# Post-norm transformer layer on one core: output projection and first norm of a query chunk moved into the next chunk's attention, result writes moved to GpSimd's queue, down products by whole chunks

## The reference

```python
Q, K, V = X @ Wq + bq, X @ Wk + bk, X @ Wv + bv
attn = softmax(q @ k.T / sqrt(16)) @ v                 # b, h, query, d
out  = attn.transpose(0, 3, 2, 1).reshape(b, s, 256)   # b, d, query, h, read as rows of 256
x = layernorm(X + out @ Wo + bo)
x = layernorm(x + ((silu(x @ Wg * sg) * (x @ Wu * su)) @ Wd) * sd)
```

## Time and profile before

| | us |
|---|---|
| median of 3 timed runs | 707.35 (707.09 to 709.0) |
| the profiled execution's own time | 709.39 |
| its span, first to last instruction | 707.6 |
| TensorE busy (matmul) | 630.2 |
| ScalarE busy | 545.9 |
| VectorE busy | 141.5 |
| GpSimd busy | 54.2 |
| mean granted clock of TensorE, as a share of full | 0.943 |

### The profile page before, as it was taken

The page is one execution under the profiler, slowest core; times in us unless marked ns, Lnnn a source line. Parts: engine busy times, 40 slices in busy tenths (PEclk is TensorE's granted clock), DMA queues, the critical chain, the costliest instruction groups (busy, mean ns, idle before and its releaser), DMA issues.

```text
span 707.6 us, 9879 instructions
## 1 busy us (share of the span) xinstructions
PE 630.2 (89%) x3938; PEld 260.8 (37%) x3938; DVE 141.5 (20%) x266; ACT 545.9 (77%) x637; POOL 54.2 (8%) x49
## 2 busy tenths in 40 slices
PE   8999999999998969998999699898959709999994
PEld 6862222222222212222222122222212108788884
DVE  6680000000000100000010000000100005856766
ACT  4639999999997969997999499899958802744442
POOL 7445000000000000000000000000012001000002
PEclk9999999999998979998999799999988958999998
DMA  7646739383749475573838293848371020000001
GB/s 226 106 64 77 78 42 102 35 100 37 87 55 96 45 79 58 66 82 42 100 53 94 31 107 36 92 51 97 39 88 12 6 38 0 1 1 30 0 30 60
DMA packets 55836, 43.21 MB, mean 61 GB/s; under 512 B 43320, under 2 KB 49336, under 8 KB 52912
## 3 DMA queue, kind: packets, MB, share of 16 engines
q1 hardware_dynamic: 54976, 42.35, 47.8%
q10 hardware_dynamic: 816, 0.26, 0.1%
HBM read 6.56 MB, written 4.33 MB: 15 GB/s over the span
## 4 chain that ended last, share of the span: by engine, by line
PE 57%; SPq 28%; DMA 5%; DVE 4%; issue 3%; ACT 2%; POOL 0%; ACTq 0%; DVEq 0%; POOLq 0%
PE ps L1043 22%; PE ps L1027 18%; SPq L286 10%; SPq L289 7%; PE ps L1111 7%; PE ps L908 5%; SPq L299 4%; SPq L297 4%; PE ps L1094 4%; SPq L312 3%; DMA q_slot<-shift 2%; PE ps L1082 2%; DMA at_dram<-attn_q 1%; ACT probs L519 1%; DVE attn_q L692 1%
## 5 line engine op out<-in xcount | busy, mean ns | idle before, releaser
L519 ACT ACTIVATE probs<-ps 128x1024 f32<-128x1024 f32 x512 | 472.0, 1317 | 54.4 <-PE ps L1027 54.2
L1043 PE MATMUL ps<-probs,v_all 128*17 128x512 f32 x2048 | 279.6, 619 | 1.7 <-DVE attn_q L692 1.1
L1027 PE MATMUL ps<-q_slot,k_slot 51*128 51x512 f32 x1024 | 230.4, 498 | 38.5 <-DMA q_slot<-shift 36.9
L1027 PEld LDWEIGHTS ps<-q_slot,k_slot 51*128 51x128 f32 x1024 | 94.5, 190 | 310.7 <-ACT probs L519 259.6
L692 DVE COPY attn_q<-ps 128x512 f32<-128x512 f32 x16 | 11.1, 691 | 490.0 <-PE ps L1043 490.0
L1043 PEld LDWEIGHTS ps<-probs,v_all 128*17 128x17 f32 x2048 | 34.3, 96 | 75.9 <-issue 64.2
L554 ACT ACTIVATE sg<-ps,sgate_c 128x512 f32<-128x512 f32 x32 | 22.1, 690 | 46.6 <-PE ps L1111 46.5
L444 POOL CAST wg<-gate 128x2048 fp32r<-128x2048 int8 x1 | 1.9, 1889 | 458.3 <-DMA q_slot<-shift 458.3
L1082 PE MATMUL ps<-wo,at 128*128 128x256 f32 x64 | 16.8, 428 | 21.9 <-DVE at L700 21.9
L531 ACT ACTIVATE x_tok<-x_tok,neg_mean,rstd 128x256 f32<-128x256 f32 x16 | 8.3, 590 | 35.1 <-DVE neg_mean L741 35.1
L1094 PE MATMUL ps<-wd,h_hi 128*128 128x256 f32 x128 | 32.2, 285 | 2.3 <-DVE r_tmp L773 2.1
(11 more groups left out here) (94 smaller groups left out, 326.5 us busy)
## 6 DMA issues: line engine op xcount, KB each, us to landing
k_slot<-k_parts SPq DMA_DIRECT2D x60, 256.0 KB
k_slot<-k_parts SPq DMA_DIRECT2D x60, 128.0 KB
q_slot<-q_parts SPq DMA_DIRECT2D x64, 64.0 KB
at_dram<-attn_q SPq DMA_DIRECT2D x64, 34.0 KB
at<-at_dram SPq DMA_DIRECT2D x8, 272.0 KB, 5.0
q_slot<-q_parts SPq DMA_DIRECT2D x64, 32.0 KB
x_tok<-in_L_attn_X SPq DMA_DIRECT2D x3, 512.0 KB, 9.0
out<-out_tmp SPq DMA_DIRECT2D x3, 512.0 KB, 3.0
```

Source lines behind the costliest of these rows:

```text
L519: nc.scalar.activation(probs[:, u % 3, 2 * p:2 * p + 2, :].rearrange("p a b -> p (a b)"), ps[:, 2 * ring:2 * ring + 2, :].rearrange("p a b ...
L1027: last = nc.tensor.matmul(ps[:, 2 * ring + half, :], k_slot[slot][base:base + ROWS, p, kt * P:(kt + 1) * P], q_slot[slot][base:base + ROWS ...
L1043: last = nc.tensor.matmul(ps[32 * hh:32 * hh + VW, ACC, :], v_all[:, kt, NQ * (s % QUADS) + hh, :], probs[:, u % 3, hh, :], start=(kt == 0 ...
```

## The change

- Result writes `move_out` are issued by GpSimd instead of SyncE. SyncE keeps `load_stack`, `load_shift` and `move_in`; `move_in(c)` moves up to the end of the iteration of the chunk's last step.
- Tokens lie otherwise on the partitions: x_tok's row (d % 4)*32 + u and column block j, c hold token j*512 + (d % 4)*128 + 32c + u, so that a chunk of queries makes whole tiles of 128 tokens. Each chunk of X is loaded by 4 DMAs of 32 partitions instead of one (two for the first) of 128; each result chunk is stored by 4.
- Chunks 0 to 2: `project_out(c, b)` runs on TensorE in units 4 and 7 of step 4c+5, and `turn_y(c, ko)` in units 4 and 7 of step 4c+6, all through bank 7. VectorE does `scale_attn`, sums, statistics and now also the scaling of the first norm after the save of step 4c+4, and both parts of the turned tile after the save of step 4c+5. GpSimd does the power between two result writes. The normed, turned chunk takes the place of Q's chunk (`qy`).
- Chunk 3: `scale_attn` after feed-forward tile 7 on VectorE, `project_out` before tile 10 and `turn_y` before tile 13 on TensorE, the VectorE parts in between.
- The feed-forward begins when attention ends. All 8 down products of a chunk run together after its 8 tiles of gate and up. `ln2_step` runs at tiles 0 to 4 of the next chunk, with two VectorE instructions instead of four in its first piece.
- The loops of the feed-forward are written out, the last stores are shared by SyncE and ScalarE.

The core of the diff:

```diff
@@ sync
+            def load_x(j):
+                for d in range(CH):
+                    sp.dma_start(x_tok[UW * d:UW * (d + 1), TPC * j:TPC * (j + 1), :], x_view[j, d]
+                                 ).then_inc(x_loaded[j], 16)
...
-                if s >= QUADS and s % QUADS == 0:
-                    move_in(s // QUADS - 1)
-                sp.wait_ge(attn_saved, s + 1)
-                move_out(s)
-            move_in(CH - 1)
+                if s % QUADS == QUADS - 1:
+                    move_in(s // QUADS)
@@ gpsimd
+            def move_out(s):
+                c = s // QUADS
+                pool.wait_ge(attn_saved, s + 1)
+                for hh in range(NQ):
+                    pool.dma_start(at_dram[c, :, NQ * (s % QUADS) + hh, :, :].rearrange("r d u -> d r u"),
+                                   attn_q[s % 2][32 * hh:32 * hh + VW, :, :]).then_inc(at_put[s % 2], 16)
...
+            for s in range(STEPS):
+                if s > QUADS and s % QUADS == 1:
+                    ln1_power(s // QUADS - 1)
+                if s == STEPS - 1:
+                    for t in range(STEPS - NSLOT, STEPS):
+                        pool.wait_ge(stack_loaded[t % NSLOT], loaded(t))
+                    nc.gpsimd.tensor_copy(wg[:], gate8[:].bitcast(i8)).then_inc(ffn_w_ready, 1)
+                    ...
+                move_out(s)
+            ln1_power(LAST)
@@ vector
+            for s in range(STEPS):
+                save_attn(s)
+                c = s // QUADS - 1
+                if s >= QUADS and s % QUADS == 0:
+                    scale_attn(c)
+                    ln1_add(c, 0)
+                    ln1_add(c, 1)
+                    ln1_stats(c)
+                    ln1_scale(c)
+                if s >= QUADS and s % QUADS == 1:
+                    ln1_parts(c, 0)
+                    ln1_parts(c, 1)
@@ tensor, attention
+                s, kt = u // UPS, u % UPS
+                c = s // QUADS - 1
+                if c >= 0 and s % QUADS == 1 and kt in (4, 7):
+                    project_out(c, kt // 7)
+                if c >= 0 and s % QUADS == 2 and kt in (4, 7):
+                    turn_y(c, kt // 7)
@@ tensor, feed-forward
+            for u in range(CH * MT):
+                c, m = u // MT, u % MT
+                if u == WO_AT:
+                    project_out(LAST, 0)
+                    project_out(LAST, 1)
+                if u == TURN_AT:
+                    turn_y(LAST, 0)
+                    turn_y(LAST, 1)
...
+                if u >= 2:
+                    pe.wait_ge(gate_up_free, u - 1)
...
+                if m == MT - 1:
+                    for b in range(c * MT, (c + 1) * MT):
                         down(b)
```

More of the change, by code:

```diff
@@ L438, in _, with ln1_power @@
                                         ).then_inc(bo_added, 1)
[L441 to L449, removed]
+            def move_out(s):
[4 more added lines that the diff above has]
+                                   attn_q[s % 2][32 * hh:32 * hh + VW, :, :]).then_inc(at_put[s % 2], 16)
+            def ln1_power(c):
                 pool.wait_ge(ln1_var, c + 1)
@@ L540, in _ @@
[L540 to L543, removed]
-            act.wait_ge(scales_loaded, 16 * 3)
[L547 to L567, removed]
@@ L1046, in prob_times_v, with project_out, turn_y @@
                 last.then_inc(pv_done, 1)
+            def project_out(c, b):
+                bank = FFN_BANK if c < LAST else 6 + b
+                if b == 0:
+                    pe.wait_ge(attn_scaled, c + 1)
+                if c == 0 and b == 0:
+                    pe.wait_ge(w_loaded[3], 16)
+                if b == 0 and c == LAST:
+                    pe.wait_ge(down_free, 2)
+                if b == 0 and c:
+                    pe.wait_ge(yt_ready, KO * c)
+                if b == 1 and c < LAST:
+                    pe.wait_ge(ln1_sum, 2 * c + 1)
+                for half in range(2):
+                    j = 2 * b + half
+                    for ko in range(KO):
+                        last = nc.tensor.matmul(ps[:, bank, half * HID:(half + 1) * HID],
+                                                at32[:, c, ko, CH * j:CH * (j + 1), :].rearrange("p d u -> p (d u)"),
+                                                wo[:, ko, :], start=(ko == 0), stop=(ko == KO - 1))
+                last.then_inc(wo_psum, 1)
+            def turn_y(c, ko):
+                bank = FFN_BANK if c < LAST else 6 + ko
+                if ko == 0:
+                    pe.wait_ge(ln1_ready, TPC * (c + 1))
+                elif c < LAST:
+                    pe.wait_ge(yt_ready, KO * c + 1)
+                for j in range(TPC):
+                    last = nc.tensor.transpose(ps[:, bank, j * P:(j + 1) * P], x_by[:, j, c, ko * P:(ko + 1) * P],
+                                               ident[:])
+                last.then_inc(yt_psum, 1)
             UNITS = UPS * STEPS
@@ L1133, in _ @@
-            ffn_chunk(0, True)
-            with pe.Fori(1, CH) as c:
-                ffn_chunk(c, False)
-            for m in range(MT - LAG, MT):
-                pe.wait_ge(h_ready, (CH - 1) * MT + m + 3)
-                down(m)
+            for u in range(CH * MT):
+                c, m = u // MT, u % MT
+                if u == WO_AT:
+                    project_out(LAST, 0)
[3 more added lines that the diff above has]
+                    turn_y(LAST, 1)
+                if m == 0 and c < LAST:
+                    pe.wait_ge(yt_ready, KO * (c + 1))
+                if u >= 2:
+                    pe.wait_ge(gate_up_free, u - 1)
+                for w, bank in ((wg, u % 2), (wu, 2 + u % 2)):
+                    for ko in range(KO):
+                        for part in range(2):
+                            last = nc.tensor.matmul(ps[:, bank, :], w[:, ko, m * P:(m + 1) * P], qy[:, c, ko, part, :],
+                                                    start=(ko == 0 and part == 0), stop=(ko == KO - 1 and part == 1))
+                last.then_inc(gate_up_psum, 1)
+                if m == MT - 1:
+                    for b in range(c * MT, (c + 1) * MT):
+                        down(b)
```

361 lines of the change are left out of this document (146 added, 215 removed).

## The result

The change makes the kernel slower: a median of 721.08 us (718.83 to 725.35, 4 runs) against 707.76 for the kernel before on the same chip, a ratio of 1.0193, 95% interval 1.0142 to 1.0244. The forecast was 639.4 us and the range ended at 670. The profiled execution took 718.83 us, with a span of 717.1.

What follows compares the result with a forecast made beforehand. SyncE's queue, with a 32.0 us period, was taken to starve attention steps wanting 29.33. Terms -43.0 + 6.9 - 32.8 + 1.0 = -67.9 took 707.35 us to 639.4, range 631 to 670.

Steps and rivals of the forecast that it cites:

- Part 1: Attention: with result writes off SyncE's queue, stacks come in time and steps take 29.33 us; -43.0 us.
- I take the spread: Attention's writes spread over four or more DMA engines, the busiest has at most 23.4 us per step, ScalarE stays the bound.
- The slower one: Rival in attention: GpSimd's issue, over 8.6 us per write, becomes the bound and the kernel gets slower; chance 0.04.
- The writes still load one engine or queue: Rival in attention: moved writes still load one DMA engine or queue, steps stay at 32 us, 675.5 us total; chance 0.12.
- Part 2: Projection and turn of chunks 0 to 2 inside attention: insertions cost 1.0 and 1.3 us per chunk, +6.9 us.
- Part 3: Last save to last down product: chunks of 22.4, 32.6, 24.0 and 24.0, 103.0 us instead of 135.8, so -32.8.
- Part 4: Kernel start: SyncE issues 11 more DMAs, so X and Wk come later; +1.0 us, bounds 0 and 3.

Runs made afterwards that it cites:

- b_sp16: The kernel before, with only SyncE's result writes of 17 partitions split into four of 16 and one of 4 per step: 654.4 us, 0.9241.
- a_sp16: The changed kernel with result writes back on SyncE, split into four of 16 partitions and one of 4 per step: 641.4 us, 0.9054.
- best2: a_sp16 with chunk 3's projection moved before feed-forward tiles 4, 6 and 10, and ScalarE making the turned tile's high part: 642.01 us, 0.9064.

## Why the prediction was wrong

**What bounds the kernel before.** It was right that a 32.0 us period of SyncE's queue starves steps of 29.33. What was missed is why: the four writes hold the queue 9.1 us and the load behind them another 2.5 because of their shape. With 16 partitions per write the same kernel has its 29.33 back (b_sp16), on the same queue. The 1.4 engines that the writes kept busy were read, and led only to the question of who else uses that engine, not to the question why 136 KB load one engine.

**Part 1, the step that failed: "I take the spread".** The price of one issue, about SyncE's 2.2 us, was right (1.9), but not that four take 9: with the hold before a later one they take up to 28 (27.4 in the rows above). The error that costs the time is that a spread divides a fixed 20 us of engine time among more engines. On GpSimd's queue the sum itself grows, from 20 to 187 us with the writes alone and 136 per step beside the loads. The bound there, 23.4 us for the busiest engine, held that sum fixed. With the measured sums, spread evenly over 16 engines, a step has (289 + 136) / 16 = 26.6 us for each, and at the share of 0.82 that the stretch shows this is 32.4 us, where the loads' period is 32.4 to 34.6. That the loads wait for engines which the writes hold is inferred from these sums; no view here shows single engines. Term: -43.0 forecast; with the insertions' -36.1, against +31.4 measured. That is 67.5 of the 81.7 us by which the forecast is off (721.08 against 639.4). The 18.4 us "of every engine" was a sum of packet times too, which can overlap, and so no firm floor for the stack.

The Trainium skill ("DMA: Bandwidth & Descriptors", "Why a DMA increments its semaphore by 16 and not by 1") takes the largest number up to 16 that divides the outer dimensions as the number of engines: 1 for 17 and 19, 9 for 18, 10 for 20. The runs sort in that way (and as even and odd), and on SyncE 17 partitions at a share of 1.4 engines and 20 at 9.4 are near it. For some copies that GpSimd issues the Trainium skill names there an exception, all engines with the partitions divided by 16 and rounded up on each; which of the two the writes of 17 take, the trace doesn't tell, since packets overlap in its shares. The Trainium skill states no price there, and the runs' is 187 against 20 us. The Trainium skill says on the same page ("Issuing engines are not separate DMA queues") that a second issuer saves only issue time and that all run on the same 16 engines; here the loads, on another queue, slowed down with the writes, which agrees.

That the shape is the cause is shown from both sides, and with this shape alone the issuer matters: on GpSimd 16, 18 and 20 partitions give 641.6, 640.99 and 640.92 us, 17 and 19 give 721.08 and 755.91; on SyncE 17 gives 679.09 and 16 or 20 give 641.4 and 641.05.

**The rivals.** The slower one named 34.3 us per step as the point where the gain is gone, and 34.3 was measured; that the kernel is 14 us slower there comes from the other terms below, and the equal number is chance. Its mechanism was not the one: an issue takes 1.9 us and not over 8.6, and GpSimd still waits 131.9 us in 16 waits for saves, so it isn't the bound. The 0.04 was too little because the price's bound "by what makes it the limit" was named and then set aside for the nearest row, which was of another queue. "The writes still load one engine or queue" was nearer in kind (transfers, not issue), but it held the total fixed too and ended at 675.5.

**Part 2, insertions: right within 0.35 us.** Forecast were 1.0 and 1.3 us. ScalarE around the two in the changed kernel:

```profile
227.22 5.61 ACT L532 ACTIVATE probs<-ps 128x1024 f32<-128x1024 f32 x6 [1.43 <-PE ps L1011]
234.08 12.02 ACT L532 ACTIVATE probs<-ps 128x1024 f32<-128x1024 f32 x13 [1.25 <-PE ps L1011]
```

In a_sp16 a step with them is 31.98 - 29.33 = 2.65 us longer, 8.0 for three chunks against 6.9. Its 15 steps take 446.5 us; the forecast's 483.0 - 36.1 is 446.9. That they agree to 0.4 is in part luck: the insertions cost 1.1 more than forecast, and the last step is 27.98 instead of 29.33.

**Part 3, after attention: right where its condition held.** It needed chunk 3's result 22 us after the last save. In the changed kernel it came at 625.79, 30 us after. The chain that ended last (start, us, what):

```profile
596.87 5.73 POOL at_dram L445 x3
602.60 11.78 issue
614.38 8.03 DMA at_dram<-attn_q
...
622.85 2.92 DMA at<-at_dram
...
625.79 0.56 DVE den L689
...
628.91 5.61 PE ps L1051 x16
```

So this stretch took 111.3 us instead of 103.0. In a_sp16, where nothing is late, the four down blocks are these (start, us, of the chain):

```profile
542.43 7.67 PE ps L1113 x64
...
574.68 8.05 PE ps L1113 x64
...
598.79 7.67 PE ps L1113 x64
...
622.48 7.21 PE ps L1113 x60
```

By their ends, and to the last down product at 629.87, the chunks take 22.6, 32.6, 23.7 and 23.4 us from the last save, 102.4 together (their sum differs by rounding); forecast were 22.4, 32.6, 24.0 and 24.0. Chunk 1's long stay is VectorE's chain of first norm, second norm and `h`, as forecast: best2, which takes the first norm out of it, brings it to 24.9.

**Part 4, start.** +2.1 us against +1.0, within its bounds of 0 and 3; in the other runs of the changed kernel +1.5 to +3.2. The first transposes wait 2.43 us for X (0.86 before) and the first products are slow, 1.20 us instead of 0.73 for two.

**The sum.** With the writes in another shape the changed kernel takes 640.9 to 641.6 us, 1.5 to 2.2 over the forecast. The 81.7 us of the error are, with rounding, 67.5 of attention, 8.3 after it, 1.1 of the start, 0.4 of rest and 4.3 because the profiled execution lay 2.0 over the median before and 2.2 under it after. With the shape mended the first two are gone: 446.5 us for the 15 steps and 102.4 after them.

## What to carry to other kernels

Before a DMA is moved to another issuer, look at what it moves: a side of 17 partitions cost the kernel before 53 us on SyncE and the changed one 80 on GpSimd, and padding or splitting it took a few lines. When four small transfers keep a queue busy 9 us at a share of 1.4 engines, that is the defect to mend, not a load to hand on. And price a transfer twice, in its issuer's time and in the engines' time, and let the second be unknown on a queue of which no row exists.

## What the runs showed of the hardware

- Four writes of 17 partitions (16 runs of 128 bytes each) by GpSimd: 160 packets per write, 187 us of engine time, landed 25.5 us after the first issue with almost nothing beside them. With 18 or 20 partitions: 32 packets per write and 2.6% or 3.1% of the engines over the run. Why such a packet costs so much is open; no run here looked into it.
- With 17 partitions a later one of GpSimd's four issues, mostly the fourth, stands up to 19.8 us, with 19 up to 25.2, but with 18 or 20 at most 0.2: the four go out in about 2.7 us. What holds it no run here shows.
- On SyncE, 17 partitions also make issue slow: 9.1 us for four, against mostly 1.8 to 1.9, at most 3.5, for four of 16 or 20.
- Loads on one queue slow down with writes on another: the stack of 20 DMAs took about 22.9 us behind SyncE's 17-partition writes, 19.7 to 21.1 with the split, and 31.8 to 38.0 beside GpSimd's. Of 18 partitions, GpSimd's writes leave it at 21.5 to 22.3.
- The shares of the DMA engines sum packets that overlap: 1.05 of 16 engines from 107.5 to 111 in the kernel before.
